# A five-stage float32 network on one core: in its 16-head attention, q and k are made unpadded and spread to head rows over DRAM, and the work beside the scores gets a new order by slots

## The reference

```python
def _self_attention(x, wq, bq, wk, bk, wv, bv, wo, bo):      # N_HEADS = 16, HEAD_DIM = 8
    q = ((x @ wq + bq) * HEAD_DIM ** (-0.5)).reshape(b, s, N_HEADS, HEAD_DIM)
    k = (x @ wk + bk).reshape(b, s, N_HEADS, HEAD_DIM)
    v = (x @ wv + bv).reshape(b, s, N_HEADS, HEAD_DIM)
    scores = jnp.einsum('bqhd,bkhd->bhqk', q, k)
    p = jax.nn.softmax(scores, axis=-1)
    o = jnp.einsum('bhqk,bkhd->bqhd', p, v).reshape(b, s, d)
    return o @ wo + bo
...
h = _layer_norm(x, ln1_g, ln1_b)
x = x + _self_attention(h, ...)
h = _layer_norm(x, ln2_g, ln2_b)        # then logits = h @ wr, two experts for each token, their slots
```

## Time and profile before

| | us |
|---|---|
| median of 3 runs | 2522.29 (2519.23 the fastest, 6669.22 the slowest) |
| the profiled execution | 2528.03 |
| its span in the profile | 2526.2 |
| attention stage in it, first load to the first load of the experts | 645.4 to 1170.1 |
| PE busy, share of the span | 80% |
| DVE busy, share of the span | 75% |
| ACT busy, share of the span | 53% |
| POOL busy, share of the span | 27% |

### The profile page before, as it was taken

One profiled execution on the slowest core, in us unless ns is written; L12 is line 12 of the kernel. 1 busy time (PEld: TensorE's weight loads), 2 busy tenths in 40 slices (PEclk: granted clock), 3 DMA queues, 4 the chain that ended last, 5 costly groups with the idle time before them and its releaser, 6 DMA issues. The chain is left out here.

```text
span 2526.2 us, 39590 instructions
## 1 busy us (share of the span) xinstructions
PE 2009.6 (80%) x12960; PEld 1109.3 (44%) x12960; DVE 1885.6 (75%) x4504; ACT 1348.4 (53%) x2902; POOL 682.2 (27%) x591
## 2 busy tenths in 40 slices
PE   5778777777389898883980674999999989999985
PEld 2233333332144444442440432656665656665653
DVE  5999999999267777751214596888887788888865
ACT  5767566662044444441433103877886478788731
POOL 1333333432002222221441033333332133333211
PEclk8989989988599999995995787999999999999997
DMA  8000000000100000002514331000000000000000
GB/s 264 0 1 5 5 4 5 5 0 9 54 3 14 16 14 18 16 17 61 163 55 116 111 111 50 1 1 1 2 1 1 1 1 1 1 1 2 1 13 21
DMA packets 81547, 73.84 MB, mean 29 GB/s; under 512 B 11284, under 2 KB 66335, under 8 KB 81120
## 3 DMA queue, kind: packets, MB, share of 16 engines
q1 hardware_dynamic: 77248, 63.26, 8.3%
q0 software_dynamic: 4096, 8.06, 0.9%
HBM read 37.80 MB, written 33.86 MB: 28 GB/s over the span
## 5 line engine op out<-in xcount | busy, mean ns | idle before, releaser
L766 DVE TENSOR_TENSOR_SCAN m_hs<-m_da,m_bu 128x1024 f32<-128x1024 f32 x128 | 303.6, 2412 | 0.3
L463 PE MATMUL m_ps_y_ps<-m_prod,m_ident 128*128 128x512 f32 x512 | 275.8, 666 | 4.9 <-DVE m_prod L776 4.9
L2766 ACT ACTIVATE l_pe<-l_ps_s,l_nbias,l_qs 128x192 f32<-128x192 f32 (+1 forms) x512 | 245.9, 490 | 13.4 <-DVE l_nbias L2938 11.5
L1271 ACT ACTIVATE a_pt<-a_ps_s 128x1024 f32<-128x1024 f32 x128 | 131.3, 1026 | 220.8 <-PE a_ps_s L1045 218.9
L373 POOL TENSOR_TENSOR m_bu<-m_dtu,m_bsb 128x1024 f32<-128x1024 f32 x64 | 151.3, 2364 | 361.9 <-ACT m_bsb L614 234.4
L1395 DVE TENSOR_REDUCE a_mpad<-a_ps_s 128x4 f32<-128x1024 f32 x128 | 156.9, 1226 | 98.0 <-PE a_ps_s L1037 96.4
L1037 PE MATMUL a_ps_s<-a_kT,a_qT 32*128 32x256 f32 x1024 | 185.3, 436 | 47.3 <-DVE a_mpad L1395 29.4
L1045 PE MATMUL a_ps_s<-a_qT,a_kT 32*128 32x256 f32 x1024 | 180.7, 429 | 1.2 <-ACT a_pt L1271 0.8
L2523 PE MATMUL l_ps_s<-l_kT,l_qT 128*128 128x384 f32 (+1 forms) x512 | 179.9, 433 | 0.0
L623 ACT ACTIVATE m_da<-m_dt,m_a_neg 128x510 f32<-128x510 f32 x256 | 168.5, 716 | 3.7 <-DVE m_hs L766 2.2
L2776 ACT COPY l_pT<-l_ps_t 128x256 f32<-128x256 f32 (+1 forms) x256 | 123.1, 481 | 71.5 <-PE l_ps_t L2533 45.3
(11 more groups left out here) (323 smaller groups left out, 4799.9 us busy)
## 6 DMA issues: line engine op xcount, KB each, us to landing
slots<-m_void SPq DMA_DIRECT2D x16, 516.0 KB, 6.1
e_xs<-slots SPq DMA_DIRECT2D x16, 258.0 KB
ys<-m_void SPq DMA_DIRECT2D x8, 512.0 KB, 6.6
e_w<-in_w SPq DMA_DIRECT2D x16, 256.0 KB, 3.5
e_yy<-ys SPq DMA_DIRECT2D x16, 256.0 KB, 5.0
m_xt<-in_L_attn_x SPq DMA_DIRECT2D x8, 256.0 KB, 3.1
x<-m_xo SPq DMA_DIRECT2D x8, 256.0 KB, 2.2
a_xn<-x SPq DMA_DIRECT2D x4, 512.0 KB, 5.4
```

Source lines behind the costliest of these rows:

```text
L463: last = pe.matmul(y_ps[h][:, :], ident[:, :], prod[s % 2][:, h, :], start=False, stop=(s == NS - 1))
L766: dve.tensor_tensor_scan(hs[s % 2][:, :, :].rearrange("p h t -> p (h t)"), da[s % 4][:, :, :, :].rearrange("p h q t -> p (h q t)"), bu[s % ...
L2766: nc.scalar.activation(pe_[u % 2][:, h, 0:nk], s_ps[u % 2][:, h * 192:h * 192 + nk], ACT.Exp, bias=nbias[:, u % 2, h:h + 1], scale=qs[b % ...
```

## The change

It does four things in `phase_attention`, and one in the stage ahead.

1. **q and k unpadded.** `wq` and `wk` are [128, 128], their columns in the order of head rows. `queries_keys(b)` is two matmuls into one bank, ScalarE adds both biases (`qk_bias`) into the tile `qk` [128, 2, 256]. queries, keys, q_bias and k_bias are gone.
2. **Spread over DRAM.** SP stores `qk` to a DRAM buffer (256 KB), waits for it, waits until the scores of the block that last used the buffer are done, and loads it back in four DMAs (j = 0 to 3), each 8 rows of 8 KB into partitions 32j to 32j + 7 of `heads` [128, 4, 2, 256], of which qT and kT are now views. The other rows are cleared once by two memsets on GpSimd, and the row of ones comes by eight small DMAs.
3. **put_max writes to `qm`**, a tile of its own, of which s2 reads.
4. **A new order by slots** on all five engines. Among other things queries_keys(b + 2) with the transpose of h2 stands in slot 6, router and counts in slot 7, no extra in slot 0; residual and the second statistics are in two slots (4 and 5); keep_logits and put_max of group 1 go to slot 0 of the next block, rows_of to slot 1, masks to slot 3; send(b - 3) comes after both powers of block b + 2.
5. **Weights ahead.** The 19 weight loads of this stage are issued in the stage before, behind its zero fills.

The diff, cut to its core:

```diff
 class AttentionWeights:
+    def load(self, sp):
+        for dst, src in self.sources:
+            sp.dma_start(dst[:], src).then_inc(self.arrived, 16)
...
+                sp.wait_ge(q_clear, 2)
+                for i in range(2):
+                    for j in range(J):
+                        sp.dma_start(kT[i][HP * j + HD:HP * j + HD + 1, :, :], w["one_row"]).then_inc(rest_in, 16)
+
+                def spread_heads(b, p):
+
+                    sp.wait_ge(qk_sb, b + 1)
+                    at_least(sp, spread[p], 16 * J * (b // 2))
+                    sp.dma_start(qk_dram[p], qk[p][:, :, :].rearrange("p i t -> p (i t)")).then_inc(bounced[p], 16)
+                    sp.wait_ge(bounced[p], 16 * (b // 2 + 1))
+                    at_least(sp, s2_mm, 8 * (b - 1))
+                    at_least(sp, m_sb, G * (b - 1))
+                    lines = qk_dram[p].rearrange("(r g) n -> r (g n)", g=G)
+                    for j in range(J):
+                        dst = heads[p][HP * j:HP * j + HD, :, :, :].rearrange("r g i t -> r (g i t)")
+                        sp.dma_start(dst, lines[HD * j:HD * (j + 1), :]).then_inc(spread[p], 16)
...
-                for k in range(0, NB // 2):
-                    store(2 * k, 0)
-                    store(2 * k + 1, 1)
+                spread_heads(0, 0)
+                spread_heads(1, 1)
+                for b in range(NB):
+                    if b + 2 < NB:
+                        spread_heads(b + 2, b % 2)
+                    store(b, b % 2)
...
+                for i in range(2):
+                    nc.gpsimd.memset(heads[i][:, :, :, :], 0.0).then_inc(q_clear, 1)
                 pool.wait_ge(w_ready, 1)
...
                 for b in range(NB):
-                    if b + 3 < NB:
-                        power(ve, rstd, var_rd, rstd_rd, b + 3)
-                    if b > 1:
-                        send(b - 2)
-                    if b + 3 < NB:
-                        power(ve2, rstd2, var2_rd, rstd2_rd, b + 3)
-                    norm_out(b)
+                    if b + 2 < NB:
+                        norm_in(b + 2)
+                    if b > 2:
+                        send(b - 3)
+                    if b > 0:
+                        norm_out(b - 1)
...
-                def queries(b):
+                def queries_keys(b):
                     pe.wait_ge(hT_sb, b + 1)
-                    for g in range(G):
-                        last = pe.matmul(ms[:, g, :], wq[:, g, :], hT[:, :], start=True, stop=True)
-                    last.then_inc(q_mm, 1)
-
-                def keys(b):
-                    pe.wait_ge(q_sb, G * (b + 1))
-                    for g in range(G):
-                        last = pe.matmul(ms[:, g, :], wk[:, g, :], hT[:, :], start=True, stop=True)
-                    last.then_inc(k_mm, 1)
+                    pe.matmul(flat[0][:, 0:T], wq[:, :], hT[:, :], start=True, stop=True)
+                    pe.matmul(flat[0][:, T:2 * T], wk[:, :], hT[:, :], start=True, stop=True).then_inc(qk_mm, 1)
...
                 def wait_s1(b, t):
                     if t == 0:
-                        pe.wait_ge(k_sb, b + 1)
+                        pe.wait_ge(spread[b % 2], 16 * J * (b // 2 + 1))
+                        if b == 0:
+                            pe.wait_ge(rest_in, 16 * 2 * J)
                     at_least(pe, max_rd, 8 * b + t)
...
+                def qk_bias(b, p):
+                    act.wait_ge(qk_mm, b + 1)
+                    at_least(act, bounced[p], 16 * (b // 2))
+                    nc.scalar.activation(qk[p][:, 0, :], flat[0][:, 0:T], ACT.Identity, bias=bq[:, 0:1])
+                    nc.scalar.activation(qk[p][:, 1, :], flat[0][:, T:2 * T], ACT.Identity, bias=bk[:, 0:1]).then_inc(qk_sb, 1)
...
-                def k_bias(b, p):
-
-                    dve.wait_ge(k_mm, b + 1)
-                    at_least(dve, s2_mm, 8 * (b - 1))
-                    dve.tensor_tensor(kT[p][:, :, :], ms[:, :, :], bk[:, :].unsqueeze(2).to_broadcast([P, G, T]), ALU.add).then_inc(k_sb, 1)
...
+                    if g == 0:
+                        dve.wait_ge(spread[p], 16 * J * (b // 2 + 1))
+                        at_least(dve, s2_mm, 8 * (b - 1))
+                    dve.tensor_tensor(qm[p][:, g, :], qT[p][:, g, :], flat[MBANK[g]][:, 0:T], ALU.add).then_inc(m_sb, 1)
```

More of the change, by code:

```diff
@@ L1150, in router, with body @@
                     last.then_inc(lg_mm, 1)
-                def body(b, p, first=False, last=0, early=False):
+                def body(b, p):
                     q = 1 - p
@@ L1489, in body @@
                         if t == 0:
-                            if last < 1:
-                                stats(b + 2)
-                            if not first and not early:
-                                pick_two(b - 2)
-                        if t == 1:
-                            if last < 2:
-                                k_bias(b + 1, q)
-                            if not first and not early:
-                                masks(b - 2)
-                        if t == 2 and not first:
-                            normalise(b - 1)
+                            if b > 0:
+                                put_max(b, p, 1)
@@ L1501, in body @@
                         if t == 3:
                             put_max(b, p, 2)
-                            if last < 1:
-                                norm_once(b + 2)
+                            if b + 2 < NB:
+                                norm_rows(b + 2)
+                            if b > 1:
+                                masks(b - 2)
                         if t == 4:
                             put_max(b, p, 3)
-                            if not first:
+                            if b + 2 < NB:
+                                norm_twice(b + 2)
@@ L1540, in _ @@
                 norm_once(1)
+                norm_rows(1)
                 norm_twice(1)
```

297 lines of the change are left out of this document (149 added, 148 removed).

## The result

The changed kernel takes 2486.18 us (median of 4 runs, 2483.44 to 2487.85) against 2522.08 for the kernel before: the ratio is 0.986, with a 95% interval of 0.9841 to 0.988. That is 35.9 us less; 28.5 were predicted, and 2486 lies inside the range. The gain is clear of the noise, but smaller than the 2% from which the prediction calls a kernel faster. (The median of the kernel before has one outlier of 6669 us in it; without it, it is 2521.87.) The profiled execution took 2487.16, its span is 2485.4.

The account below looks back on a forecast made before the run. It took a TensorE-VectorE loop of 2.91 us per slot as the bound, leaving 4.3 us a block to win. Terms -7.8 + 2 - 3.4 - 19.4 - 0.4 + 0.5 = -28.5 gave about 2494 us, range 2474 to 2516.

Parts of the forecast that it names:

- start, first load to first exponential: Start of attention: earlier hn 5.5, shorter way to s1 0.4, block 1's queries 1.9; together 7.8 us less.
- block 0: First block: spread of block 1 late and clock rising later, against one keys and queries less; loses 2 us.
- blocks 1 and 2: Blocks without sends before the change: win 1.7 us each, 3.4 in all.
- blocks 3 to 13: Eleven blocks: 25.8 us each against 27.56, 19.4 less in all.
- The stall: Slot 1, 3 to 6 us behind the first send: 1.11 us a block; kept at 1.0, moved to slot 4.
- a rival with 2483: Stall beside the sends goes or meets slack: 11 us more saved, about 2483; chance 0.14.
- TensorE's extras: TensorE work above the 2.91 us loop: slots 7 and 0 lose 1.03 each; new slots 6 and 7 are 0.4 and 0.37 above.
- VectorE's chains: VectorE work ahead of the row maximum: slot 0 0.3 above the loop, slot 4 0.2, slots 1 and 2 0.1 each.
- The rival with longer chains: VectorE's chains 0.2 us longer per slot, 1.6 a block: about 2515; chance 0.14 shared with loads in a row.
- The spread: Store of qk and four loads: fourth load there 3.4 us into slot 0, needed at 6.2 in slot 2; no wait.
- The margin of 2.8: Time in us between the fourth spread load's landing and the first s1 needing it, in slot 2.
- The rival in which the loads don't overlap: Four spread loads of 2.0 us in a row, 1.5 late, 14 times: about 2515; chance 0.14 shared with poorer order.

Follow-up runs that it names:

- kernel with the late loads: Changed kernel with the four loads of the spread issued one slot later from block 2 on; 2524.57 us, ratio 1.0018.
- last kernel: Changed kernel further ordered, with TensorE filler at the start and in block 0, q/k matmuls ahead of weigh, spread store in two halves; 2464.76 us, ratio 0.9789.
- kernel with 16-row loads: Changed kernel with spread loads one slot later, as two DMAs of 16 rows instead of four of 8, output wrong; 2515.57 us, ratio 0.9944.
- kernel with filler: Changed kernel, further ordered, with unread matmuls on TensorE during the first spread and behind the first six scores; 2494.74 us, ratio 0.9867.

## Why the prediction was right, and where not

The fair base is the second profile of the kernel before (span 2517.8). The attention stage, first load to first load of the experts, took 516.0 us in it and takes 483.1 now: 32.9 less. Against the first profile, from which the prediction's terms were read, it is 524.8 - 483.1 = 41.7 less. The 35.9 of the medians against 32.9 lie within what executions of one kernel differ by. By the steps of the prediction, measured against the second profile:

| step | predicted | measured |
|---|---|---|
| start, first load to first exponential | -7.8 | -5.7 |
| block 0 | +2 | +3.3 |
| blocks 1 and 2 | -3.4 | -4.0 |
| blocks 3 to 13 | -19.4 | -24.6 |
| block 14 | -0.4 | -1.7 |
| last block and end | +0.5 | -0.2 |
| sum | -28.5 | -32.9 |

- **The stall** was misread, on both sides of the sum. It was taken as part of the kernel before (1.11 a block) and kept in the changed kernel (1.0). It was in neither usual run. As it was kept, it nearly cancelled, and that is luck: two signs of being right, exponentials 25.8 us apart and a stall of about 1 us near slot 4, did not come (24.33, and none). Had it been taken as gone, which was a rival with 2483, the sum would have counted 11 us that the usual run never had. That 2486 lies nearer to this 2483 than to the forecast of 2494 doesn't speak for it. The sign was in the prediction's own numbers: the profiled execution was 5.7 us above the median, and "the difference moves with it" was written over it without asking what those 5.7 us were.
- **TensorE's extras** were right: slots 6 and 7 are 3.30 and 3.28 (predicted 3.3 and 3.28), slot 0 is free of its 1.03, and leaving half of the matmuls out of the kernel before gave 0.86 per slot (0.96 expected).
- **VectorE's chains** were sized too long by 0.1 to 0.2 in slots 0, 2 and 4: predicted 3.2, 3.0 and 3.1, measured 2.99, 2.91 and 2.99. Their kind is right, as the statistics put back into slot 4 show. Without the stall the prediction has a block of 24.8, measured 24.33; times 11 this is the 5 us by which blocks 3 to 13 beat their term. The rival with longer chains is out.
- **The spread** is the step that failed without being felt. A load of 8 rows was priced at 2.0, from a row of a load over 128 rows, and half the engines at "under 0.5". Shown are 5.8 to 6.1 us from the first issue to the last increment in blocks 3 to 13, 2.1 to 2.4 more than the prediction's 3.7. The margin of 2.8 covered it to the last 0.1 to 0.5, so it cost nothing there, which is luck too. The rival in which the loads don't overlap had the mechanism, four loads one behind the other, which was set aside with a chance of at most 0.14; only its landing, 7.7 in slot 0, was too late: it is 5.7 in block 7. The prediction put the point at which the whole gain is gone at 4.8 us beyond its landing of 3.4. The kernel with the late loads lands 4.2 beyond it, and the gain is gone already, since behind most of its waits the clock fell. Waits of 0.9 us in the last kernel did not lower it, so short ones cost only themselves.
- **The start.** hn comes 8.65 us after the first load, 1.1 earlier than priced; the GpSimd memsets took 3.62 instead of 4.5. But the first spread took 2 us more, and the 1.9 us counted for the queries of block 1 were 0.3: from the first s1 to the first exponential it takes 32.5 us against 32.9. Block 0 paid for both unknowns, as foreseen: s1 of slot 2 waited 1.67 us for the spread of block 1, and the clock rose 10 us later than before, counted from the first load. Its slots are 3.95, 5.23 and 4.12.
- **The weights ahead** carry the start. Alone they are worth 8.3 by the medians and 11.7 by the profiles, not 5.5.

Open: why semaphores come late beside the sends in the call on one chip and in one execution of an earlier call. The changed kernel itself was not run on that chip. The kernel with 16-row loads has its order in slots 3 and 4 and lost 3.0 us a block there, the kernel before about 1.1, and it was 12.6 us ahead of it by the medians. So the gain may be much smaller on such a chip; that is argued from the slots, not shown.

## What to carry to other kernels

Before you explain a stall, ask whether the profiled execution is a usual one: compare its time with the median, and profile again if the two differ by as much as the stall is worth. Count the rows of a transfer, not only its bytes: the same 256 KB need 6.2 us in loads of 8 rows and at most 4.4 in loads of 16. A gap in front of TensorE is paid nearly twice if the clock falls behind it, and a few matmuls that nobody reads, put where TensorE would wait anyway, keep it up: here they were worth 7.9 us.

## What the runs showed of the hardware

- What TensorE signals to ScalarE, VectorE or itself can come 1 to 2 us late, beginning some 3 us after the first of four indirect sends of GpSimd. On one chip all three profiled executions had it; of the eleven other profiles only the first one of the kernel before had it in full.
- Behind 13 of 14 waits of 1.5 to 1.9 us TensorE's granted clock fell from 1.00 to 0.50, and was back after about 3 us in ten cases and about 7 in three. Behind three waits of 0.9 us it stayed at 1.00. In block 0 of the kernel with filler one idle time of 1.4 us had a fall behind it. The Trainium skill ("TensorE: Matmul & The Clock Gate", Part 1) has the throttled state as the default that activity releases; these rows agree.
- Four loads of 8 rows of 8 KB put their last increment 5.8 to 6.1 us after the first issue, two of 16 rows 3.8 to 4.1; from the end of the last packet to the last increment it is 1.6 and 1.3 us of these, in the block shown of each.
- Beside the GpSimd memset of 2048 columns, VectorE's scaling of 128x128 weights took 1.81 us, where 128x512 took 0.43 before.
